# First phase of a decoder kernel: one weight store moved up, low rows awaited later, projections and rotations in pairs

## The reference

```python
# self attention of layer 0, on xn = layernorm(x)
qkv = xn @ w_qkv.T                      # 16 heads of 32
q = q * cos + rotate_half(q) * sin      # the same for k
scores = q @ k.T * 32 ** -0.5           # kept where 0 <= q_pos - k_pos < 64
x = x + (softmax(scores) @ v) @ w_out.T

# cross attention of layer 0, on hn = layernorm(x)
q = hn @ Wq.T + bq; k = ctx @ Wk.T + bk; v = ctx @ Wv.T + bv
p = softmax(clip(where(mask, q @ k.T / sqrt(32), -10000), -50, 50))
delta = rs * ((p @ v) @ Wo.T + bo)
x = x + layernorm(delta) * gamma + beta
```

## Time and profile before

| what | us |
|---|---|
| runs of the kernel before | 3356.50, 3351.46, 3356.14 (median 3356.14) |
| the profiled execution's own time | 3357.66 |
| span of that execution in the profile | 3355.7 |
| first phase, from the start to PE's last output projection | 829 |
| PE busy over the span | 3070.7 (92%) |
| DVE, ACT, POOL busy over the span | 2319.1, 1596.8, 803.4 |

### The profile page before, as it was taken

How to read it: one execution, slowest core, us unless ns; L and a number is a source line. 1 busy time by engine, 2 the same in 40 slices (tenths; PEclk the granted TensorE clock), 3 DMA queues, 4 the chain that set the end, 5 groups by cost and what they waited for, 6 DMA issues and landing times. The chain is left out here.

```text
span 3355.7 us, 61560 instructions
## 1 busy us (share of the span) xinstructions
PE 3070.7 (92%) x22897; PEld 2477.5 (74%) x22897; DVE 2319.1 (69%) x4413; ACT 1596.8 (48%) x3648; POOL 803.4 (24%) x1000
## 2 busy tenths in 40 slices
PE   6999999997899699999999859889899879999999
PEld 5666666664788588888888746657566678888888
DVE  4565656655666588888888666868686767777776
ACT  3233333322322355555555426657575755555555
POOL 1211221221444211111111153332323012222222
PEclk8999999999899799999999969999999979999999
DMA  6224323320111477777777531212120032222222
GB/s 258 102 87 159 126 101 114 126 101 4 55 58 33 170 242 246 243 243 241 241 243 244 205 112 64 83 44 74 35 71 7 16 128 82 73 73 70 73 73 70
DMA packets 145099, 401.95 MB, mean 120 GB/s; under 512 B 39200, under 2 KB 48032, under 8 KB 131952
## 3 DMA queue, kind: packets, MB, share of 16 engines
q1 hardware_dynamic: 106448, 323.37, 28.3%
q0 software_dynamic: 18976, 50.45, 5.1%
q10 hardware_dynamic: 19456, 25.18, 2.1%
HBM read 344.16 MB, written 54.76 MB: 119 GB/s over the span
## 5 line engine op out<-in xcount | busy, mean ns | idle before, releaser
L1450 POOL DMA_INDIRECT xg<-normed_rows,idx x128 | 126.6, 989 | 644.6 <-PE psum L1532 590.1
L2618 POOL TENSOR_TENSOR mixf<-act 128x256 f32<-128x256 f32 x128 | 143.4, 1121 | 497.0 <-DVE act L2879 497.0
L174 POOL TENSOR_SCALAR ve<-mv 128x1 f32<-128x1 f32 x112 | 34.9, 311 | 863.3 <-DVE mv L767 597.8
L1547 PE MATMUL psum<-xT_hi,wgu_hi 128*128 128x192 f32 (+1 forms) x1536 | 228.4, 271 | 2.4 <-DVE xT_lo L1592 2.4
L1547 PE MATMUL psum<-xT_lo,wgu_hi 128*128 128x192 f32 (+1 forms) x1536 | 223.3, 268 | 0.0
L1547 PE MATMUL psum<-xT_hi,wgu_lo 128*128 128x192 f32 (+1 forms) x1536 | 222.8, 267 | 0.0
L1586 DVE TENSOR_TENSOR wgu_lo<-wgu,wgu_hi 128x1408 fp32r<-128x1408 f32 x128 | 202.4, 1622 | 22.3 <-ACT wgu_hi L1474 22.2
L1547 PEld LDWEIGHTS psum<-xT_hi,wgu_hi 128*128 128x128 f32 (+1 forms) x1536 | 190.6, 182 | 27.0 <-ACT wgu_hi L1474 21.2
L1487 ACT ACTIVATE eth<-psum 128x192 f32<-128x192 f32 (+1 forms) x192 | 63.2, 329 | 301.3 <-PE psum L1547 301.2
L1989 ACT ACTIVATE scratch<-psum,smin 128x512 f32<-128x512 f32 x256 | 173.7, 685 | 62.6 <-DVE smin L2379 60.0
L1547 PEld LDWEIGHTS psum<-xT_lo,wgu_hi 128*128 128x128 f32 (+1 forms) x1536 | 190.8, 183 | 0.0
(11 more groups left out here) (427 smaller groups left out, 8678.7 us busy)
## 6 DMA issues: line engine op xcount, KB each, us to landing
wgu<-in_w_gu_dram SPq DMA_DIRECT2D x64, 1408.0 KB, 6.0
w_slot<-w_split SPq DMA_DIRECT2D x21, 2048.0 KB, 8.5
wd<-in_w_d_dram SPq DMA_DIRECT2D x64, 512.0 KB, 8.7
w_raw<-in_w_dram SPq DMA_DIRECT2D x128, 256.0 KB, 2.6
expert_out<-yo ACTq DMA_DIRECT2D x64, 256.0 KB, 5.2
w_slot<-w_split SPq DMA_DIRECT2D x28, 512.0 KB, 4.5
wd<-in_w_d_dram SPq DMA_DIRECT2D x64, 192.0 KB, 9.0
w_split<-w_slot SPq DMA_DIRECT2D x4, 2048.0 KB, 12.2
```

The costliest lines, as they stand in the source:

```text
L1450: pool.indirect_dma_start(out=xg[b][0:w, t, :], out_offset=None, in_=rows, in_offset=bass.IndirectOffsetOnAxis(ap=idx[b][0:w, t:t + 1], ax ...
L1547: ins = pe.matmul(bank(2 + m)[0:w, gu * CAP:(gu + 1) * CAP], wgu2[b][wp][:, gu, kc, m0:m0 + w], xT2[b][xp][:, kc, :], start=(i == 0 and kc ...
L2618: pool.tensor_tensor(mixf[:, g % LAG, :], act2[:, g % LAG, 0, :], act2[:, g % LAG, 1, :], ALU.add).then_inc(sy["f_mix"], 1)
```

## The change

It makes four edits, all in `phase1`. SP stores Q's split parts right after the first context load, ahead of the raw XQ pieces and the other late weights, and no longer after them. PE's `queries_keys` does two projections and then the two rotations of the pair before. For sequences 1 to 7, `values(i, 0)` moves ahead of the last two rotations; in sequence 0 it stays behind them. For XQ, PE waits for the high rows only, does the first two products of chunks 0 and 1 in banks 6 and 7, then waits for the low rows and does the third product of both.

```diff
             load_ctx(0)
+            store_unit(Q)
             for n in range(KC):
                 load_raw(XQ, n, n + 1, "w1b_in")
...
                 if i == 0:
-                    for u in (Q, K, V, XQ):
+                    for u in (K, V, XQ):
                         store_unit(u)
...
-            def products(out, lhs_of, rhs_of, order):
-                for m, (lp, rp) in enumerate(order):
+            def products(out, lhs_of, rhs_of, order, first=0, end=3):
+                for m in range(first, end):
+                    lp, rp = order[m]
...
             def queries_keys(i):
-                for c in range(2 * KC + 1):
-                    if c < 2 * KC:
-                        if c >= 2:
-                            pe.wait_ge(sy["qk_raw_ready"], due("qk_raw_ready", i, c - 1))
-                        weights_in(Q if c < KC else K, i, c % KC)
-                        from_columns(bank(2 + c % 2)[:, 0:S], Q if c < KC else K, c % KC).then_inc(sy["qk_proj"], 1)
-                    if i == 0 and c == 1:
+
+                for n in range(KC + 1):
+                    for c in (2 * n, 2 * n + 1):
+                        if c < 2 * KC:
+                            if c >= 2:
+                                pe.wait_ge(sy["qk_raw_ready"], due("qk_raw_ready", i, c - 1))
+                            weights_in(Q if c < KC else K, i, c % KC)
+                            from_columns(bank(2 + c % 2)[:, 0:S], Q if c < KC else K, c % KC
+                                         ).then_inc(sy["qk_proj"], 1)
+                    if i == 0 and n == 1:
                         pe.wait_ge(sy["w1_in"], n_early * 16)
-                    if c >= 1:
-                        pe.wait_ge(sy["qk_raw_ready"], due("qk_raw_ready", i, c))
-                        if c >= 3:
-                            pe.wait_ge(sy["rope_ready"], due("rope_ready", i, c - 2))
-                        pe.matmul(bank(4 + (c - 1) % 2)[:, 0:S], rot[:], qk_raw[:, c - 1, :], start=True,
-                                  stop=True).then_inc(sy["rot_psum"], 1)
+                    if n == KC and i >= 1:
+                        values(i, 0)
+                    for c in (2 * n - 2, 2 * n - 1):
+                        if c >= 0:
+                            pe.wait_ge(sy["qk_raw_ready"], due("qk_raw_ready", i, c + 1))
+                            if c >= 2:
+                                pe.wait_ge(sy["rope_ready"], due("rope_ready", i, c - 1))
+                            pe.matmul(bank(4 + c % 2)[:, 0:S], rot[:], qk_raw[:, c, :], start=True,
+                                      stop=True).then_inc(sy["rot_psum"], 1)
...
                 queries_keys(i)
-                values(i, 0)
+                if i == 0:
+                    values(i, 0)
...
                 rows_to_cols(h, normed_attn(i), turned_attn(i))
+                pe.wait_ge(sy["colsT_ready"], turned_attn(i) + NT)
+                weights_in(XQ, i, KC - 1)
+                for c in range(2):
+                    from_columns(bank(6 + c)[:, 0:S], XQ, c, 0, 2)
                 pe.wait_ge(sy["colsT_lo"], turned_attn(i) + NT)
-                weights_in(XQ, i, KC - 1)
-                for c in range(KC):
-                    if c >= 2:
-                        pe.wait_ge(sy["xq_ready"], due("xq_ready", i, c - 1))
+                for c in range(2):
+                    from_columns(bank(6 + c)[:, 0:S], XQ, c, 2, 3).then_inc(sy["xq_psum"], 1)
+                for c in range(2, KC):
+                    pe.wait_ge(sy["xq_ready"], due("xq_ready", i, c - 1))
                     from_columns(bank(6 + c % 2)[:, 0:S], XQ, c).then_inc(sy["xq_psum"], 1)
```

More of the change, by code:

```diff
@@ L558, in products, with from_columns @@
                 return ins
-            def from_columns(out, u, c):
+            def from_columns(out, u, c, first=0, end=3):
                 return products(out, lambda p, kc: w_slot[u % 2][:, c, p, kc * P:(kc + 1) * P],
-                                lambda p, kc: hT2[p][:, kc, :], ((0, 0), (1, 0), (0, 1)))
+                                lambda p, kc: hT2[p][:, kc, :], ((0, 0), (1, 0), (0, 1)), first, end)
             def weights_in(u, i, n):
```

## The result

The changed kernel takes 3337.56 us (median of 6 runs, 3336.05 to 3341.18), the kernel before 3356.03 (6 runs, 3351.46 to 3357.21). The ratio is 0.9947, with a 95% interval of 0.9937 to 0.9957: 18.5 us less, where 18.4 were forecast. The profiled execution took 3336.63 us, with a span of 3334.9.

A forecast was written before the change was run, and what follows sets the result against it. PE, busy 92% of the span, bounds the kernel; only its idle or half-clock time in the first phase can be won. 9.5 + 5.4 + 3.5 = 18.4 us off the 3356.14 median gives 3338, range 3331 to 3349.

The forecast's parts named there:

- The store: Sequence 0: Q's store lands at 21.7, ACT's 11.85 us wait goes, values start at 38.0; 9.5 us gained.
- two waits of 1.3: Sequence 0 projections: PE waits twice, 1.3 us each, for DVE's split of K, at about 22.5 and 27.5.
- High rows first: Cross queries, all eight sequences: PE starts 0.83 us earlier on high rows; 0.67 gained each, 5.4 us in all.
- Pairs: Projection stretch of sequences 1 to 7: scores reached 0.6 us earlier, 0.5 taken for each, 3.5 us in all.
- The values cover the last two: Sequences 1 to 7: the values fill PE's time ahead of the last two rotations; within the 0.5 us a sequence.
- The clock: Rival, sequence 0: the 1.3 us gaps or the longer one let the clock fall; about 4 us lost, 3342, chance 0.12.
- a bound of 3 us below its forecast: Sequence 0: values and cross queries also come out of half clock, some 3 us more gain than 9.5.
- DVE was not late: Rival, sequences 1 to 7: DVE's chain grows by up to 3.5 us beside POOL; 7 us lost, 3345, chance 0.10.
- The slower outcome: Rival: DVE's chain ends so late that the clock falls in every sequence; 3.2 us lost in seven, 3360, chance 0.05.
- The rival of a late store: Rival, sequence 0: Q's store lands with the late weights at 39.1, the long stop stays; 3347, chance 0.05.
- parts two and three: Cross queries with high rows first, 5.4 us, and pairs in sequences 1 to 7, 3.5 us; together 8.9.

The follow-up runs named there:

- e4: The changed kernel with the third and fourth chunk of the cross queries in banks 4 and 5: 3334.08 us, ratio 0.9933 to the kernel before.
- e6: The changed kernel with values(i, 0) of sequences 1 to 7 put back behind the last two rotations: 3394.85 us against 3397.22 for the kernel before, ratio 0.9995.
- e1: The kernel before with only Q's store moved ahead of the late weights: 3341.01 us, ratio 0.9956 to the kernel before.
- e2: The changed kernel with Q's store put back behind the late weights: 3351.39 us, ratio 0.9986 to the kernel before.
- e7: The changed kernel with Q's store behind the raw cross query pieces and two more weights, ahead of the last three: 3376.23 us, ratio 0.9940 to the kernel before.

## Why the prediction was right

**The store.** The mechanism held in each step, the sizes nearly. Landing 21.7 forecast, 21.9 measured; two waits of 1.3, measured 1.31 and 1.24; values at 38.0, measured 38.62. The first rotation at 21.6 was met to 0.01, but by chance: in the five traces with pairs in sequence 0 it starts between 21.10 and 22.33. From it to the values it took 17.0 us where the working has 16.4 (17.0 in e4 and e6 too). About half of that is in the four projections behind the waits, 1.48 us each for 1.40, and the rest in rope and split, behind which PE went on 2.33 and 2.26 us after the rotation for 2.13. Counted from the first projection, the gain is 9.3 against a term of 9.5. e1 and e2 show both halves of it: the landing is what ended the long stop, and the pairs take 4.5 to 5.5 us of the gain back (34.13 and 33.13 against 38.62), where the prediction had said "about 4 more" without them.

**High rows first: right mechanism, wrong size.** The term was 0.67 a sequence and 5.4 in all. It is 0.47 in sequences 1 to 7 and, by e1, whose sequence 0 ran at full clock with the long wait, 0.66 in sequence 0 (9.39 to 8.73); 3.9 in all. The start came 0.83 earlier, as worked out. I had taken 0.117 us for each matmul at once; after a stop of PE the first eight take 1.20 instead of 1.10, a tenth that my stepping left out behind the first stop, and there is now one stop more, ahead of the third chunk. Those two tenths are the difference, and e4, which takes the second stop away, gets 0.37 back.

**Pairs: 0.6 a sequence against 0.5.** Seven sequences give 4.2 against 3.5. My stepping said 0.6 for PE, and I had taken less since I thought that DVE's first minimum, 0.45 sooner in the stepping, would set it. It came 0.5 sooner and set nothing. e6 shows how much hung on one short sentence of the prediction, "The values cover the last two": without that cover the edit is a loss, of 1.7 us a sequence against the kernel before.

**The clock.** By their terms the three parts give 9.3 + 3.9 + 4.2 = 17.4 us. The last output projection of the phase comes 20.56 us sooner, with 0.3 lost at the start; so 3.4 us are left over. Nearly all of them (1.65, and 10.95 - 9.39 = 1.56) are two stretches of sequence 0 in which the kernel before ran partly at half clock and this one did not, as windows show. First before, in the attention and in the cross queries (busy us of each engine, then the granted clock):

```profile
72.00:78.00 6.00, 4.30 (x34) 2.91 (x38) 3.27 (x7) 1.95 (x10) 0.00 (x0) 0.72 1.04 382
103.40:107.00 3.60, 3.57 (x17) 3.57 (x18) 2.87 (x6) 0.47 (x1) 2.56 (x5) 0.53 0.06 16
```

Then after, in the same two places:

```profile
66.00:70.00 4.00, 2.95 (x29) 2.16 (x28) 2.18 (x6) 0.38 (x1) 0.00 (x0) 1.00 0.93 332
91.80:94.30 2.50, 2.50 (x21) 2.50 (x22) 2.43 (x6) 0.00 (x0) 0.52 (x2) 1.00 0.48 181
```

The first is chance: e4 has the changed kernel's code there and took 38.44 where that took 36.67, and e1 took 38.00. The second is not shown to be the change's doing. In all eight kernels with the short wait the stage took at most 8.75; of the two with the long wait, before and e1, only one fell to half clock. In e1 the same wait of 1.74 us left the granted clock at 1.00 (88.8 to 92.0 us), and the first eight matmuls took 1.20 where they had taken 1.96:

```profile
88.86 1.20 PE L557 MATMUL psum<-hT_hi,w_slot 128*128 128x256 f32 x8 [1.74 <-DVE hT_lo L818]
```

A wait of this length brings the clock down at times and at times not; what decides it, the runs don't show. The prediction had both only as a bound of 3 us below its forecast. That the forecast met the median so closely is then partly luck: terms 1.0 us too high in sum, against 3.2 us of clock that it had left out, and a median difference (18.5) that lies 2.3 below that of the traces (20.8) by the scatter of the runs.

**The rivals.** The clock did not fall behind the 1.3 us waits of sequence 0; it fell during the longer idle ahead of the values (0.93 from 36.5 to 38.6 us, 0.50 from 38.6 to 41), where it was below 1.00 before too (0.78 from 44.0 to 47.6, 0.79 from there to 50.0). DVE was not late: one sum of eight took 0.80 (242.91) in the stretch shown, where three took 0.71 to 0.87 before, and it lay beside the values. The slower outcome needed 2.1 us lost per sequence; e6 is that mechanism let loose, with 1.7 lost and 3.3 where half clock was added, and it cost all that the other parts bring. The rival of a late store was priced too low: "parts two and three alone give 8.9: 3347" leaves out that the pairs then put four ropes and four splits behind the late landing. e2 is that case, and its median was 3351.

## What to carry to other kernels

Look for whoever waits for a store that frees a buffer, and put that store ahead of loads that nobody needs yet; the first room is the distance between its landing and the first wish to write there, and behind it may lie a second one, until the engine on the critical path needs what that write lets through (e7: landing 5.1 us past the wish, 0.7 lost). Putting dependent short products in pairs is no gain in itself: it delays the first of them for the next engine, and in sequences 1 to 7 it paid only with other work over the last ones. After moving a wait to an earlier part of the operands, see which buffer stops the stage next; here it was a bank, and two idle ones stood beside it.

## What the runs showed of the hardware

In the cross queries PE's first eight matmuls after a stop took 1.20 us at full clock, the same eight without a stop 1.10, in every sequence (188.63 has it inside its sixteen, 191.80 by itself). A term worked out from matmuls in a run is too large by 0.1 for each stop that stands in the new order. In the projections of sequence 0 it is not so plain: at 25.42, without a stop, eight took 1.17, as many as behind the stop at 23.94 (1.18); why is open.

Behind a wait of 1.74 us the granted clock fell to 0.5 in one trace (103.43, before) and stayed at 1.00 in another (88.86, e1); behind the seven waits of 1.57 before it never fell. In e6 it fell in two of seven sequences behind waits of 1.41 and 0.48, and the stretch took 1.5 us longer each time.

Stages without a nearby clock change repeated to within 0.1 us between sequences, kernels and two chips, while the medians of the kernel before differed by 41 us between the chips (mean granted clock of its runs 0.960 and 0.953). Differences of a few us are better read from stages than from whole times.
